# Third-layer weights and first input fetched during the last block of the second stage; squares moved to GpSimd, first scaling moved to VectorE

## What is computed

```python
q, k = rmsnorm(x @ Wq), rmsnorm(x @ Wk)              # per head: x / sqrt(mean(x^2) + eps) * w
v = x @ Wv
gate = softplus(einsum('bthd,hd->bht', k, u_n) / sqrt(D))
scores = einsum('bihd,bjhd->bhij', q, k) * scale - dist * omega_eff * gate   # causal
y = einsum('bhij,bjhd->bihd', softmax(scores), v) @ Wproj
x = layernorm(x + y)
h = silu(tlin(x, w1)) * tlin(x, w2)                  # tlin(x, w, s) = (x @ w.T) * s
h = gelu(tlin(h, h1))
h = gelu(tlin(h, h2))
out = layernorm(x + tlin(h, w3))
```

## Time and profile before

| | us |
|---|---|
| three runs | 3411.91, 3413.56, 3414.53 (median 3413.56) |
| the profiled execution | 3411.78, of which the span is 3410.0 |
| attention | about 0 to 2215 of the span |
| ffn_up | about 2217 to 2923 |
| ffn_down | about 2925 to 3410 |
| busy PE, DVE, ACT, POOL | 3176.4, 1737.3, 1791.5, 1371.6 |

### The profile page before, as it was taken

The page is one execution under the profiler, slowest core; times in us unless marked ns, Lnnn a source line. Parts: engine busy times, 40 slices in busy tenths (PEclk is TensorE's granted clock), DMA queues, the critical chain, the costliest instruction groups (busy, mean ns, idle before and its releaser), DMA issues. The chain is left out here.

```text
span 3410.0 us, 45907 instructions
## 1 busy us (share of the span) xinstructions
PE 3176.4 (93%) x15472; PEld 2461.2 (72%) x15472; DVE 1737.3 (51%) x4112; ACT 1791.5 (53%) x3057; POOL 1371.6 (40%) x1188
## 2 busy tenths in 40 slices
PE   3899999999999999999999999989999999899998
PEld 3667767667677677676676676668888888688887
DVE  6566566566666665665666666352222222232322
ACT  1467676666666676666667667742222222222222
POOL 3365665655655655656556556711111110000000
PEclk7799999999999999999999999989999999899999
DMA  1322422422423324224224225242222221222120
GB/s 52 88 63 54 92 61 58 94 61 52 101 49 87 72 46 94 61 56 93 61 54 99 55 62 145 57 116 87 87 87 86 88 86 39 101 71 74 39 73 19
DMA packets 196522, 249.12 MB, mean 73 GB/s; under 512 B 67264, under 2 KB 95040, under 8 KB 196160
## 3 DMA queue, kind: packets, MB, share of 16 engines
q1 hardware_dynamic: 196288, 246.19, 28.1%
HBM read 84.86 MB, written 43.52 MB: 38 GB/s over the span
## 5 line engine op out<-in xcount | busy, mean ns | idle before, releaser
L431 POOL TENSOR_TENSOR e_lo<-e_all,e_hi 128x512 fp32r<-128x512 f32 (+1 forms) x832 | 1030.8, 1246 | 804.8 <-ACT e_all L693 723.9
L693 ACT ACTIVATE e_all<-ps_s,bias 128x512 f32<-128x512 f32 (+3 forms) x1280 | 787.3, 622 | 175.6 <-POOL e_lo L431 78.4
L686 ACT ACTIVATE e_hi<-ps_s,bias 128x512 fp32r<-128x512 f32 (+1 forms) x832 | 558.9, 672 | 251.8 <-PE ps_s L998 159.6
L885 DVE TENSOR_REDUCE maxes<-ps_m 128x1 f32<-128x512 f32 x768 | 515.3, 683 | 206.6 <-PE ps_m L978 205.3
L978 PE MATMUL ps_m<-k_ext,q_max 128*128 128x512 f32 (+3 forms) x1280 | 471.2, 388 | 61.9 <-DVE maxes L885 30.1
L997 PE MATMUL ps_s<-q_twice,k_split 128*128 128x512 f32 (+3 forms) x1280 | 480.5, 375 | 34.2 <-ACT e_all L693 29.3
L998 PE MATMUL ps_s<-q_ext,k_ext 128*128 128x512 f32 (+3 forms) x1280 | 471.8, 369 | 0.0
L1031 PE MATMUL ps_v<-e_lo,v_main 128*66 128x512 f32 (+1 forms) x832 | 434.2, 522 | 19.2 <-POOL e_lo L431 19.1
L978 PEld LDWEIGHTS ps_m<-k_ext,q_max 128*128 128x128 f32 x1280 | 247.3, 194 | 222.1 <-DVE maxes L885 80.4
L882 DVE CUSTOM_DVE_ANT_0 ps_m<-ps_m,mask_row 128x128 f32<-128x128 f32 (+3 forms) x512 | 250.7, 494 | 172.7 <-PE ps_m L978 170.4
L1015 PE MATMUL ps_v<-e_all,v_full 128*66 128x512 f32 (+2 forms) x896 | 324.7, 444 | 0.0
(11 more groups left out here) (248 smaller groups left out, 5892.4 us busy)
## 6 DMA issues: line engine op xcount, KB each, us to landing
q_twice<-q_max SPq DMA_DIRECT2D x256, 128.0 KB, 2.3
yt<-y_out SPq DMA_DIRECT2D x128, 130.0 KB
k_ext<-kq_hi SPq DMA_DIRECT2D x128, 128.0 KB, 2.3
q_max<-kq_hi SPq DMA_DIRECT2D x128, 128.0 KB, 2.4
k_split<-kq_hi SPq DMA_DIRECT2D x128, 128.0 KB, 2.4
k_split<-kq_lo SPq DMA_DIRECT2D x128, 128.0 KB, 2.4
q_ext<-kq_lo SPq DMA_DIRECT2D x128, 128.0 KB, 2.4
hidden<-gelu SPq DMA_DIRECT2D x64, 256.0 KB, 2.0
```

What stands on the lines that cost most here:

```text
L431: on.tensor_tensor(e_lo[:, i % LO_RING, off:QB], e_all[:, u_ % E_RING, off:QB], e_hi[:, i % HI_RING, off:QB].bitcast(F32), ALU.subtract).t ...
L686: nc.scalar.activation(e_hi[:, i % HI_RING, off:QB], ps_s[u_ % 2][:, off:QB], ACT.Exp, bias=by).then_inc(hi_done, 1)
L693: nc.scalar.activation(e_all[:, u_ % E_RING, off:QB], ps_s[u_ % 2][:, off:QB], ACT.Exp, bias=by).then_inc(ex_done, 1)
L885: nc.vector.tensor_reduce(maxes[:, qt, kc:kc + 1], ps_m[m % 2][:, 0:width], AX.X, ALU.max).then_inc(mx_free, 1)
```

## The change

Three separate things are done.

1. In attention the squares are made by POOL. ACT's copy now signals `pj_free`. Eight `square` steps per pair (128x512 each: one of the four column groups, eight tiles of tokens) read `raw` alone, and DVE has eight smaller sums in place of four. For the first pair the first square waits for DVE's constants (`s_const`), since `sq` holds constants until then. The next four squares wait for the sums of the four before.
2. The eight `first scale` multiplications of y_first go from POOL to DVE, at the same place in the list of steps. In ffn_up the split of Wproj is done in two halves, the first after the first y_hi, the second after the second.
3. The buffers of ffn_down's stage (now eight, not two) and of a_in are allocated over weights of ffn_up that are no longer read (w1 and w2 over the stage, Wproj over a_in), and SP loads them in the last block of ffn_up: a_in at its start, the eight rows of h2 after its first layer. The identity for transposes is kept from attention. In ffn_down SP loads only the scales and w3.

```diff
@@ attention_steps
-        for i in range(TT // TQ):
-            at(t0 - 1.72 + 0.030 * (TQ * i + 3) + 0.03, "sum", p, i)
+        for i in range(4):
+            at(t0 - 1.44 + 0.05 * i, "square", p, i)
+            at(t0 - 1.38 + 0.05 * i, "sum", p, i)
+            at(t0 - 1.22 + 0.04 * i, "square", p, i + 4)
+            at(t0 - 1.16 + 0.04 * i, "sum", p, i + 4)
@@ attention, gpsimd
+                if step[0] == "square":
+                    p, i = step[1:]
+                    col, rows = (q_cols(0), q_cols(1), k_cols(0), k_cols(1))[i % 4], slice(i // 4 * HT, (i // 4 + 1) * HT)
+                    gp.wait_ge(pj_free, TT * p + HT * (i // 4 + 1))
+                    if p == 0 and i == 0:
+                        gp.wait_ge(s_const, 1)
+                    if p or i >= 4:
+                        gp.wait_ge(ss_done, 8 * p + i - 3)
+                    nc.gpsimd.tensor_tensor(sq[:, i % 4, :, :], raw[:, rows, col:col + D], raw[:, rows, col:col + D], ALU.mult).then_inc(sq_done, 1)
@@ attention, scalar
-                    nc.scalar.activation(raw[:, t, :], work_bank(step)[:, 0:WCOLS], ACT.Copy).then_inc(pj_raw, 1)
+                    nc.scalar.activation(raw[:, t, :], work_bank(step)[:, 0:WCOLS], ACT.Copy).then_inc(pj_free, 1)
@@ attention, vector
-                    nc.vector.tensor_tensor(sq[:, t % (2 * TQ), :], work_bank(step)[:, 0:CB], raw[:, t, 0:CB], ALU.mult).then_inc(pj_free, 1)
+                    dve.wait_ge(sq_done, 8 * p + i + 1)
+                    nc.vector.tensor_reduce(sumsq[:, i % 4, i // 4 * HT:(i // 4 + 1) * HT], sq[:, i % 4, :, :], AX.X, ALU.add).then_inc(ss_done, 1)
...
+                if step[0] == "first scale":
+                    c = step[1]
+                    if c == 0:
+                        dve.wait_ge(kept.first_load, 16 * 4 * OC)
+                    nc.vector.tensor_tensor(kept.y_first[:, c, :], kept.y_first[:, c, :], kept.r_first[:, c, :], ALU.mult).then_inc(kept.first_scaled, 1)
@@ ffn_up, sync, sp_body of the last block
+                sp.wait_ge(y_used, OC * NBLK)
+                for s in stored:
+                    sp.wait_ge(s, 1 + 16 * (OC // AR))
+                sp.dma_start(later.a_in[:], a_dram[:, 0:NTOK].rearrange("(k p) n -> p k n", p=P)).then_inc(later.a_load, 16)
+                sp.wait_ge(l1_full, OC * NBLK)
+                for r in range(OC):
+                    sp.dma_start(later.stage[r][:], h2_w[r * P:(r + 1) * P, :]).then_inc(later.staged[r], 16)
@@ ffn_up, scalar, first_x
                     split_y(i, c)
+                    if c == 0:
+                        act.wait_ge(wp_load, 16)
+                    if c < 2:
+                        nc.scalar.activation(wp_hi[:, 4 * c:4 * (c + 1), :], wp_in[c], ACT.Copy).then_inc(wp_first, 1)
                     weights(c)
@@ ffn_down, sync
-            for i, (w, cut) in enumerate(rows):
-                if i >= 2:
-                    sp.wait_ge(wt_full, 2 * (i - 1))
-                sp.dma_start(stage[i % 2][:], w[cut, :]).then_inc(staged[i % 2], 16)
-                if i == 1:
-                    load_a(sp, 0)
+            for i in range(KC):
+                sp.wait_ge(wt_full, 2 * (slot_of(OC + i) + 1))
+                sp.dma_start(stage[slot_of(OC + i)][:], w3_w[i * P:(i + 1) * P, :]).then_inc(staged[slot_of(OC + i)], 16)
```

More of the change, by code:

```diff
@@ L83, in count_of, with rooms @@
     return n * sum(m in modes for m in MODES) + sum(m in modes for m in MODES[:v])
+def rooms(nc, ctx, *uses):
+    for n, use in enumerate(uses):
+        with ExitStack() as short:
+            stack = ctx if n == len(uses) - 1 else short
+            yield [stack.enter_context(nc.sbuf_tensor(name, shape, dt)) for name, shape, dt in use]
 class Kept:
@@ L94, in room @@
         def room(*uses):
-            for n, use in enumerate(uses):
-                with ExitStack() as short:
-                    stack = ctx if n == len(uses) - 1 else short
-                    yield [stack.enter_context(nc.sbuf_tensor(name, shape, dt)) for name, shape, dt in use]
+            return rooms(nc, ctx, *uses)
         (self.ident, self.sums), = room([("ident", [P, P], F32), ("sums", [P, 2, TT], F32)])
         stage = [(f"up_stage{i}", [P, 8 * P], F32) for i in range(STAGES)]
-        first, late, (self.xt_hi, self.xt_lo) = room(
+        first, late, (self.h2_hi,), (self.xt_hi, self.xt_lo) = room(
             [*stage, ("up_y_first", [P, OC, NTOK], F32)],
             [("up_stages", [P, STAGES, 8 * P], F32), ("p_lo", [P, OC, NTOK], F32R)],
+            [("h2_hi", [P, OC, HID], F32R)],
             [("xt_hi", [P, KC, T], F32R), ("xt_lo", [P, KC, T], F32R)])
@@ L124, in __init__ @@
         self.y_out_done = [sem(f"y_out_done{i}") for i in range(2)]
+class KeptLater:
+    def __init__(self, nc, ctx):
+        stages, (self.b_lo,), firsts = rooms(nc, ctx, [(f"dn_stage{i}", [P, 8 * P], F32) for i in range(OC)],
+                               [("b_lo", [P, OC, NTOK], F32R)],
+                               [(name, [P, KC, HID], F32R) for name in ("w1_hi", "w1_lo", "w2_hi", "w2_lo")])
+        self.stage = stages
+        self.w1_hi, self.w1_lo, self.w2_hi, self.w2_lo = firsts
+        (self.a_in,), (self.wp_hi, self.wp_lo) = rooms(nc, ctx, [("a_in", [P, OC, NTOK], F32)],
+                                                       [("wp_hi", [P, OC, C], F32R), ("wp_lo", [P, OC, C], F32R)])
+        self.staged = [ctx.enter_context(nc.semaphore(f"dn_staged{i}")) for i in range(OC)]
+        self.a_load = ctx.enter_context(nc.semaphore("dn_a_load"))
 def attention_steps():
@@ L623, in _ @@
                         take_rest(gp, nc.gpsimd, n, v)
-                if step[0] == "first scale":
-                    c = step[1]
-                    if c == 0:
-                        gp.wait_ge(kept.first_load, 16 * 4 * OC)
-                    nc.gpsimd.tensor_tensor(kept.y_first[:, c, :], kept.y_first[:, c, :], kept.r_first[:, c, :], ALU.mult).then_inc(kept.first_scaled, 1)
         @block.scalar
@@ L1062, in weight_rows, with ffn_up @@
         + [(h1_w, slice(i * P, (i + 1) * P)) for i in range(OC)]
-def ffn_up(nc, yt_dram, recip_dram, x, x1_dram, w1_w, w1_s, w2_w, w2_s, h1_w, h1_s, a_dram, kept):
+def ffn_up(nc, yt_dram, recip_dram, x, x1_dram, w1_w, w1_s, w2_w, w2_s, h1_w, h1_s, a_dram, kept, later, h2_w):
     ctx = ExitStack()
@@ L1087, in ffn_up @@
         p_hi, p_lo = sb("p_hi", [P, OC, NTOK], F32R), kept.p_lo
-        wp_hi, wp_lo = sb("wp_hi", [P, OC, C], F32R), sb("wp_lo", [P, OC, C], F32R)
+        wp_hi, wp_lo = later.wp_hi, later.wp_lo
         y_in = sb("y_in", [P, YR, NTOK])
@@ L1247, in weights @@
                 nc.scalar.activation(out, src, ACT.Copy).then_inc(wt_hi, 1)
-            act.wait_ge(wp_load, 16)
-            for k in range(2):
-                nc.scalar.activation(wp_hi[:, 4 * k:4 * (k + 1), :], wp_in[k], ACT.Copy).then_inc(wp_first, 1)
             def split_y(i, c):
@@ L1346, in normalise_x, with out_weights @@
                 last.then_inc(ln_done, 1)
-            for k in range(2):
+            def out_weights(k):
                 dve.wait_ge(wp_first, k + 1)
@@ L1375, in first_x @@
                 for c in range(OC):
+                    if i == 0 and c == 0:
+                        out_weights(0)
                     split_y(i, c)
+                    if i == 0 and c == 1:
+                        out_weights(1)
                     if i == 0:
@@ L1460, in _, with ffn_down @@
             over_blocks(pe, first_x, body)
-def ffn_down(nc, a_dram, x1_dram, h2_w, h2_s, w3_w, w3_s, out):
+def ffn_down(nc, a_dram, x1_dram, h2_s, w3_w, w3_s, out, kept, later):
     ctx = ExitStack()
@@ L1498, in ffn_down @@
         made = sem("dn_made")
-        staged = [sem(f"dn_staged{i}") for i in range(2)]
+        staged, a_load = later.staged, later.a_load
         wt_full = sem("dn_wt_full")
@@ L1520, in ffn_down, with slot_of @@
         table = [(h2_hi, h2_lo, i, False) for i in range(OC)] + [(w3_hi, w3_lo, i, False) for i in range(KC)]
-        rows = [(h2_w, slice(i * P, (i + 1) * P)) for i in range(OC)] + [(w3_w, slice(i * P, (i + 1) * P)) for i in range(KC)]
         NW = 2 * len(table)
+        def slot_of(item):
+            return item if item < OC else item - OC // 2
         def over_blocks(eng, split_a, body):
@@ L1677, in _ @@
         def _(pe):
-            pe.wait_ge(made, 2)
             pe.sem_inc(l3_full, 1)
```

67 lines of the change are left out of this document (29 added, 38 removed).

## The result

The changed kernel takes 3361.8 us (median of 4 runs, 3360.51 to 3363.94), the kernel before 3414.05 us (4 runs on the same chip): a ratio of 0.9847, 95% interval 0.983 to 0.9865. The profiled executions have spans of 3410.0 and 3362.1 us, 47.9 apart; the other 4 are the spread between runs of one kernel.

What follows compares the result with a forecast made beforehand. It took TensorE, busy 93% of the span, as the bound, so other engines' edits count only where it stands still. Terms 8.9 + 4 + 5 - 0.7 + 9.6 = 26.8 us off 3411.78 gave 3385.0 us, range 3368 to 3401.

Steps and rivals of the forecast that it cites:

- Start of attention: First pair's projections: PE's 9.33 us wait for DVE's square goes; gain 8.9 us, between 5.3 and 10.3.
- At the most it is as before: Upper bound for the 14 projections after the wait at attention's start: 1.41 us each, 19.8 us in all.
- Squares in the steady state: 15 pairs of attention: POOL's idle time covers the squares, PE regains waits for DVE's maxima; ends +13.5 and -112 us.
- I take 4: Gain in us costed for the 15 steady pairs, from PE waiting less for DVE's maxima.
- the limit: Sign in the steady pairs: the prediction is wrong if the pairs change by more than 1 us.
- rival C: Steady pairs: DVE, queued behind ACT's copy, was the hidden brake; 27 us in place of 4, 3362 us; chance 0.08.
- Last head: Last head of attention: eight scalings leave POOL for DVE, so ACT waits less; gain 5 us, between 2.0 and 7.4.
- mutual blocking: Last head: DVE products with two SBUF inputs and POOL products hold each other up; 5.4 us come back as POOL time.
- Start of ffn_up: Start of ffn_up: ACT's first y_hi must wait for the last store of y_out; loss 0.7 us (0 to 1).
- Start of ffn_down: Start of ffn_down: early loads leave the second scale last, PE's first third-layer matmul comes sooner; gain 9.6 us (8.2 to 9.8).
- PE itself shows only 0.3: Argument against rival C: in the steady pairs PE's own wait for DVE's maxima is only 0.3 us.

Runs made afterwards that it cites:

- experiment 2: Three kernels: the changed kernel with DVE's waits for ACT's copy put back, with added DVE work like the squares', and with both: 3357.2, 3363.3 and 3361.5 us.
- experiment 4: The changed kernel with each square made twice on POOL, 16 instructions a pair instead of 8: 3401.1 us, ratio 0.9973 to the kernel before.
- experiment 8: Changed kernel, POOL's weight products later, ACT splitting a before the scales' wait: 3359.4 us; also later maxima 3374.9; each again with later weight loads: 3316.3, 3329.1.

## Why the prediction was right or wrong

*Start of attention*: right in its mechanism, 10.7 for 8.9, though 0.4 above its upper end of 10.3 (the 1/sqrt itself began 10.1 us earlier). PE took 1.07 us a tile, the lower end, for the 1.16 that I took, and a square 1.01 for 1.10. That the wait cost more than its 9.33 us, through the clock behind it, I had not seen; it was hidden in "At the most it is as before".

*Squares in the steady state*: wrong, and the step that failed is the term "I take 4", with its upper end of 13.5: the pairs gained 20.7 us, 17.4 at full clock, and so changed by more than the 1 us each that I had set as the limit. The mechanism was the one named, PE waiting for DVE's maxima, and rival C came near its size, 27 us for 20.7, and to the time, 3362 for 3361.8. But that is luck: C's cause was the queue of waits behind ACT's copy, and experiment 2 shows that putting these waits and the work of the squares back costs nothing that can be measured. Three things went wrong in the step. I took the 0.3 us of PE itself and added up to 0.9 with the 0.6 of its weight loads, but these are one wait, and the load has its whole length:

```profile
831.34 0.19 PEld L978 LDWEIGHTS ps_m<-k_ext,q_max 128*128 128x128 f32 x1 [0.65 <-DVE maxes L885]
```

It stands behind another sum of 1.21 us (at 829.48) and the maxima after it. The window of the earlier trace rows ended at 835.8, and the two waits of 0.36 and 0.41 us at 840.9 and 841.5 lie just behind it; together 1.4 us a pair stood at these two places, of which small sums gained 1.05. Over the whole of pair 5 the loads wait 4.5 us for these maxima. And I costed what the change did to the place of the work, and not that it cut the sums in two; that had no line in my sum, and it was most of the steady gain. DVE's waits for POOL's squares were nothing, as costed: 6.0 us in all, the whole of it in the first pair. That POOL's idle time covers the squares was right, and experiment 4 puts the edge of that cover between 8 and 16 squares a pair.

*Last head*: right, 6.4 for 5. The mutual blocking that I feared is in the trace: while both run, DVE's eight products take 1.62 us each, where others take 0.69, and POOL's nine e_lo 1.65 for 1.28. In the timeline:

```profile
2159.97 14.87 POOL L457 TENSOR_TENSOR e_lo<-e_all,e_hi 128x512 fp32r<-128x512 f32 x9 [2.04 <-ACT e_all L723]
...
2160.75 12.96 DVE L934 TENSOR_TENSOR up_y_first<-up_y_first,up_r_first 128x512 f32<-128x512 f32 x8
```

POOL loses 3.3 us over its nine e_lo (14.87 less 9 x 1.29), not 5.4, and only 1.0 of it reaches ACT. DVE pays the larger share and has nothing else to do. The rule of the Trainium skill ("SBUF — State Buffer", "Who interferes with whom") holds in direction, but its full price doesn't show here: if each product of 0.69 us and each e_lo of 1.29 shut the other out for its whole length, eight of both would take 15.8 us, and the eight products were over in 12.96.

*Start of ffn_up*: 0.2 to 0.3 us lost for 0.7; DVE's split of one half took 1.23 us and ACT's y_hi waited for the last store, as written.

*Start of ffn_down*: right, 9.5 for 9.6, and the second scale is what comes last, 3.62 us after its issue; experiment 8 took 1.1 us more by not waiting for it.

The chance of 0.88 for faster held. The range's lower end, 3368, left out most of C, whose chance I had set at 0.08 because "PE itself shows only 0.3".

## What to carry to other kernels

Where a fast chain of short instructions shares an in-order engine with other work, look at the longest single instruction put between them, against the slack of the banks, and not only at the engine's busy time or its waits: here 94 us of added work and 210 us of added waiting cost nothing, and sums longer by 0.5 us each cost 11 to 13 us over 15 pairs at full clock (6 to 21 by the medians). Sum PE's waits by releaser over the whole program before picking a window, and read them on the weight loads too, without adding the two where they are one wait. And price a wait of PE at more than its length where several stand close together, since the clock often fell behind them here.

## What the runs showed of the hardware

Where PE stood still near units 56 to 63, mostly for about 1 and 2 us one after the other, the granted clock fell in 95 of 180 pairs, a fall costing some 1.7 us; with most of the second wait gone it fell in none of 36. Pairs with the same two waits (0.8 and 2.0) took a fall or did not, and which pairs take a fall is not fixed in the program. After 8.9 us of standing still the clock was at half for 5.7 us.

A DVE product with two inputs in SBUF beside a running POOL product took 1.62 us instead of 0.69 in the mean and 1.78 at most, so DVE lost 0.93 to 1.09 us to a POOL instruction of 1.29; POOL lost 0.37 in the mean.
